# Two cross-attentions of a decoder: early key loads, row normalisation on another engine, one edge product for two batches

## The chip, the cores and the metric

The kernel runs on one core of a Trainium2 chip. It is one program of 47,756 instructions on five engines: TensorE (PE in the profile; PEld are its weight loads), VectorE (DVE), ScalarE (ACT), GpSimd (POOL) and SyncE (SP), which here only issues transfers. The metric is the time of one execution on the device in microseconds, lower is better.

## The reference

Two decoder layers work on x of 2 batches x 512 tokens x 512 features; each has self-attention, cross-attention to a context of 2 x 1024 x 512, and a mixture of experts. Every sublayer gets the layer norm of x, and its result is added to x.

```python
x = x + attn0(layernorm(x))            # 16 heads of 32, rotary, causal
x = x + xattn0(layernorm(x), ctx)
x = x + moe0(layernorm(x))             # 8 experts, best 2
x = x + attn1(layernorm(x))
x = x + xattn1(layernorm(x), ctx)
x = x + moe1(layernorm(x))             # 32 experts, best 6, and a shared one

# xattn0: 16 heads of 32. qdq rounds each row to 255 steps of its own scale
q = qdq(xn) @ qdq(wq).T + bq
k, v = split(ctx @ wkv.T + bkv)
out = qdq(softmax(q k / sqrt(32)) v) @ qdq(wp).T + bp

# xattn1: 16 heads of 128. Context rows 0..256 ("image") have their own weights
q = rms(xn @ q_w + q_b) * nq_s
k = [rms(ctx[:257] @ ki_w + ki_b) * nki_s, rms(ctx[257:] @ k_w + k_b) * nkt_s]
v = [ctx[:257] @ vi_w + vi_b, ctx[257:] @ v_w + v_b]
out = (attention over image rows + attention over text rows) @ o_w + o_b
```

## The kernel before

Each sublayer is a sequence of stages. A stage (class `Stage`, line 47) owns buffers and semaphores; leaving it clears the semaphores and sets a barrier over all engines. In a stage a block holds one hand-written program per engine; the order of the work is the order of these programs, and they meet only in semaphores. An engine that waits holds everything behind it in its program. P is 128, D 512, KC = 4 (chunks of 128 features), NT = 8 (row tiles of 128 tokens). The eight banks of PSUM are `g.ps`.

**Self-attention's output stage** (`self_attention`, 228 to 258) multiplies by wo, adds to x, and takes each row tile's mean and deviation (`g.mv`, `g.rstd`), so that a later layer norm is one instruction per tile. Its block has programs for PE, DVE and ACT only.

**First cross-attention, projections** (`project_cross0`, 873). First it calls `layer_norm` (139) with `turn=False`: a stage of its own in which DVE normalises the eight tiles into `g.xt` (line 173) and SP runs `load_first` (922): key half of wkv, context chunk 0, three biases, value half of wkv, wq, wp, context chunk 1. After its barrier comes the main block:

- PE: keys of context chunks 0 and 1 (`key`, line 1113, eight units of 4 products, four banks), after `wkv_loaded` has counted both halves of wkv; then the turns of the rounded wq and rows (1131), row scales (1144), queries (1153), values of chunks 0 and 1 (1122), the turns of wp, keys and values of chunks 2 and 3. The context sits in a ring of two chunks.
- ACT: per key unit the bias (1058) into one of two slots of `raw`, then the high part (1052); in between the rounded tiles become bf16 (`whole`, 1064): one of wq after each of the first four keys, two row tiles after each of the next four. Then it copies the turned tiles (1068).
- POOL: ones for a later pack (792), then for each unit the low part, raw minus high (976).
- SP: per unit a store of the high and of the low part (941, 943). A slot of `raw` is free only when both have landed (`held`, 1045).
- DVE: rounds wq (reduce 984, then 995 and 998 per tile), then the eight normalised tiles, then wp.

**Second cross-attention** (`cross_attention1`, 1961). Products that need full precision are done as three (`split_matmul`, 2077): both operands are split into a high part, as the reduced-precision type takes it, and the rest. `project_kq1` (2085) makes keys and queries of 16 heads in six units per head, each stored by SP (2154); POOL adds up the squares (2330). At the end SP waits until all stores have landed (2179 and 2180), then the stage closes. `project_v1` (2343) makes the values in four groups of 512 columns. Its opening: PE adds the squares over the partitions (2432, 2435), ACT takes roots (2463, 2467), then ACT splits image and text weights (2446) and DVE makes their low parts (2480). A group has 16 units of 128 context rows: four of image rows, two edge units, one per batch, and ten of text rows. The edge unit's tile holds context row 256, the last image row, and 127 text rows; the tile is multiplied by the text weights into its bank and, a second time, by the image weights into bank 4 + b, of which only the first row is used:

```python
for kind, bank in [(m, t % 4)] + ([(0, 4 + b)] if kb == EDGE else []):
    for k in range(KC):
        mm = split_matmul(...)
```

DVE adds the bias (2496), for an edge unit also the one image row (2500); ACT makes the high part (2459), POOL the low part (2523), SP stores both (2391). PE waits for DVE's row four units back, ACT for the store four units back. Before the last group SP issues the first loads of keys and queries for the attention (`load_kq`, 1979), into the buffer from which `project_kq1` stored.

## Time and profile before

| | us |
|---|---|
| Median of 3 runs (lowest, highest) | 3056.08 (3052.72, 3059.84) |
| Profiled execution, its time / its span | 3058.46 / 3056.3 |
| PE busy | 2733.5 (89% of the span) |
| PE weight loads | 2009.2 (66%) |
| DVE / ACT / POOL busy | 1484.0 / 1298.6 / 1105.3 |
| DMA | 521.87 MB, 171 GB/s on average |
| Granted PE clock, mean | 0.939 of 2.4 GHz |

The profile is of one execution. All times within it count from the span's start. In a timeline row stand the start, the length, the engine, the line of the code, the operation, what is written from what, and how often in a row; in brackets how long the engine had idled and what released it. "SPq" is the issuing of a transfer, not the transfer. A clock of 0.50 is 1.2 GHz. The matmuls overlap, so the spacing of their starts tells more than their lengths. The first cross-attention's projections run from about 282 to 432 us, the second's keys and queries from 1300 to 1595, and its values from 1595 to 1813.

### The profile page before, as it was taken

The page shows a single profiled execution, that of the slowest core. Times are in us where ns is not written, and L with a number is a line of the kernel's source. Part 1 is how long each engine was busy: PE and PEld are TensorE (multiplying, and loading weights), DVE is VectorE, ACT ScalarE, POOL GpSimd, SP SyncE. Part 2 cuts the span into 40 slices and gives each one's busy share as a digit, 9 for nine tenths or more (in the row PEclk, how much of TensorE's full clock was granted, in tenths as well). Part 3 has the DMA queues.
Part 4 walks back from the last instruction along what each step waited for, and adds up shares of the span by engine and source line. Part 5 has one row for each costly group of instructions (what it writes and reads, how often), then busy time and mean ns, then how long its engine had stood idle before and what let it go on. Part 6 is the DMA issues. An engine that isn't in the chain of part 4 may idle for free. (4 is left out here: it accounts for less than half of the span.)

```text
span 3056.3 us, 47756 instructions
## 1 busy us (share of the span) xinstructions
PE 2733.5 (89%) x15758; PEld 2009.2 (66%) x15758; DVE 1484.0 (49%) x2664; ACT 1298.6 (42%) x2923; POOL 1105.3 (36%) x1019
## 2 busy tenths in 40 slices
PE   7887899996699498889989989999998879999987
PEld 5653443432588375478877879999997647777762
DVE  5575436776211427588864337667663441111115
ACT  2462424554111136466652238888882202222220
POOL 2352225664111205335543445555551011122116
PEclk9898999998699799989999999999999889999998
DMA  2332424310499414066666764444431129999986
GB/s 93 83 84 94 154 84 100 67 32 4 171 324 321 135 42 104 23 207 244 230 233 204 213 216 171 173 172 172 176 147 59 51 67 341 344 345 344 338 257 211
DMA packets 318128, 521.87 MB, mean 171 GB/s; under 512 B 35474, under 2 KB 168466, under 8 KB 309812
## 3 DMA queue, kind: packets, MB, share of 16 engines
q1 hardware_dynamic: 290036, 450.00, 45.3%
q0 software_dynamic: 13280, 43.53, 4.6%
q10 hardware_dynamic: 14688, 26.75, 2.4%
q8 instruction: 70, 1.15, 0.2%
q14 instruction: 54, 0.44, 0.0%
HBM read 365.39 MB, written 129.50 MB: 162 GB/s over the span
## 5 line engine op out<-in xcount | busy, mean ns | idle before, releaser
L1788 PE MATMUL ps<-moe_blocks_xgt,moe_blocks_w 128*128 128x128 f32 (+1 forms) x3000 | 356.1, 278 | 9.2 <-DMA moe_blocks_b1s<-rb_cols 5.8
L1788 PEld LDWEIGHTS ps<-moe_blocks_xgt,moe_blocks_w 128*128 128x128 f32 (+1 forms) x3000 | 343.2, 185 | 13.7 <-issue 9.9
L2718 POOL TENSOR_TENSOR normed<-normed,xa_core_rinv 128x257 f32<-128x257 f32 (+1 forms) x256 | 260.4, 1039 | 214.3 <-DVE xa_core_rinv L2642 214.3
L1859 DVE COPY moe_blocks_y<-ps 128x512 f32<-128x512 f32 x102 | 70.5, 692 | 451.5 <-PE ps L1770 451.5
L1770 PE MATMUL ps<-moe_blocks_w,moe_blocks_ht 128*128 128x512 f32 (+1 forms) x612 | 279.8, 594 | 0.0
L596 POOL TENSOR_TENSOR sa_w<-sa_w,sa_core_rinv 128x256 f32<-128x256 f32 (+3 forms) x128 | 159.4, 1253 | 225.5 <-DVE sa_core_rinv L543 225.0
L1735 POOL COPY moe_blocks_idx<-moe_index 128x1 uint32 (+1 forms) x102 | 18.6, 183 | 556.0 <-PE ps L1761 428.8
L2698 ACT ACTIVATE normed<-normed,xa_core_nmax,xa_rq 128x257 f32<-128x257 f32 (+1 forms) x256 | 206.7, 809 | 4.2
L2330 POOL TENSOR_TENSOR normed<-normed 128x512 f32<-128x512 f32 x96 | 150.5, 1568 | 116.8 <-DVE normed L2283 116.8
L1809 ACT ACTIVATE moe_blocks_xgt<-ps 128x512 f32<-128x512 f32 x102 | 60.9, 597 | 299.6 <-PE ps L1761 299.6
L833 DVE TENSOR_REDUCE xa_nmax<-ps 128x1 f32<-128x1024 f32 x128 | 149.2, 1216 | 58.9 <-PE ps L824 58.9
L1770 PEld LDWEIGHTS ps<-moe_blocks_w,moe_blocks_ht 128*128 128x128 f32 (+1 forms) x612 | 109.1, 192 | 98.5 <-issue 98.5
L2657 DVE CUSTOM_DVE_ANT_0 normed<-ps,xa_rk 128x257 f32<-128x257 f32 (+1 forms) x256 | 164.6, 682 | 14.4 <-PE ps L2082 10.5
L573 ACT ACTIVATE sa_w<-ps,sa_core_nmax 128x128 f32<-128x128 f32 (+3 forms) x256 | 132.3, 523 | 82.5 <-DVE sa_core_nmax L539 81.3
L2688 ACT ACTIVATE xa_core_pt<-ps 128x512 fp32r<-128x512 f32 x256 | 139.0, 595 | 65.4 <-PE ps L2620 65.0
L2648 DVE TENSOR_TENSOR xa_core_pt<-ps,xa_core_pt 128x512 fp32r<-128x512 f32 x256 | 164.5, 684 | 3.5 <-ACT xa_core_pt L2688 3.5
L2080 PE MATMUL ps<-xa_core_pt,xa_core_v 128*128 128x256 f32 x512 | 155.5, 304 | 0.1
L498 PE MATMUL ps<-identity,sa_w 128*128 128x128 f32 x640 | 125.7, 308 | 30.8 <-DVE normed L552 16.5
L1838 ACT ACTIVATE moe_blocks_ht<-ps,moe_blocks_b1s 128x128 f32<-128x128 f32 (+1 forms) x237 | 68.9, 361 | 179.7 <-PE ps L1788 179.7
L2082 PE MATMUL ps<-xa_core_pt,xa_core_v 128*128 128x256 f32 x512 | 145.1, 283 | 0.0
L2081 PE MATMUL ps<-xa_core_pt,xa_core_v 128*128 128x256 f32 x512 | 144.9, 283 | 0.0
L2523 POOL TENSOR_TENSOR xa_v_parts<-normed,xa_v_parts 128x512 fp32r<-128x512 f32 x64 | 89.5, 1400 | 126.2 <-ACT xa_v_parts L2459 126.2
(347 smaller groups left out, 6678.0 us busy)
## 6 DMA issues: line engine op xcount, KB each, us to landing
moe_blocks_w<-L_ffn_rw SPq DMA_DIRECT2D x79, 704.0 KB, 5.7
moe_blocks_w<-L_ffn_rw SPq DMA_DIRECT2D x79, 512.0 KB, 6.8
k_parts<-xa_parts SPq DMA_DIRECT2D x64, 512.0 KB, 3.3
v_parts<-xa_v_parts SPq DMA_DIRECT2D x128, 256.0 KB, 2.7
xa_parts<-k_parts SPq DMA_DIRECT2D x32, 1024.0 KB, 6.7
xa_core_v<-v_parts SPq DMA_DIRECT2D x32, 1024.0 KB, 4.9
moe_blocks_w<-L_ffn_w SPq DMA_DIRECT2D x23, 1408.0 KB, 7.6
moe_y<-moe_blocks_y ACTq DMA_DIRECT2D x102, 256.0 KB, 6.3
```

What stands on the lines that cost most here:

```text
L596: nc.gpsimd.tensor_tensor(prob[:, 2 * s:2 * s + 2, 0:n], prob[:, 2 * s:2 * s + 2, 0:n], rinv[:, s, :, 0:1].to_broadcast([P, 2, n]), ALU.mu ...
L833: nc.vector.tensor_reduce(self.nmax[:, i % 2, m:m + 1], g.ps[:, bank:bank + 2, :].rearrange("p a n -> p (a n)"), X_AXIS, ALU.max, negate=T ...
L1770: mm = nc.tensor.matmul(g.ps[:, 6 + s % 2, :], ht[0:fn, s % 2, f, :], w2s[s][0:fn, f, :], start=(f == 0), stop=(f == NF - 1))
L1788: mm = nc.tensor.matmul(g.ps[0:fn, 2 + s % 2 + 2 * half, f * P:(f + 1) * P], w1s[s][:, k, half * F + f0:half * F + f0 + fn], xgt[:, s % 2, ...
L2080: nc.tensor.matmul(out, lhs_high, rhs_high, start=start, stop=False)
L2081: nc.tensor.matmul(out, lhs_high, rhs_low, start=False, stop=False)
L2082: return nc.tensor.matmul(out, lhs_low, rhs_high, start=False, stop=stop)
L2330: nc.gpsimd.tensor_tensor(sums[:, u * 512:(u + 1) * 512], sums[:, u * 512:(u + 1) * 512], sq[:, u % 2, :], ALU.add).then_inc(summed, 1)
L2648: nc.vector.tensor_tensor(pt[:, slot, 1, 4 * half:4 * half + 4, at:at + P], g.ps[:, 4 + half, :].rearrange("p (m q) -> p m q", m=4), pt[:, ...
L2657: ins = nc.vector.tensor_tensor_reduce(prob[:, n % PR, lo:hi], s_ps(n)[:, lo:hi], rk[:, b * CTX + lo:b * CTX + hi], 1.0, -3.4e38, ALU.mult ...
L2698: ins = nc.scalar.activation(prob[:, n % PR, lo:hi], prob[:, n % PR, lo:hi], ACT.Exp, scale=rq[:, t:t + 1], bias=nmax[:, n % PR, m:m + 1], ...
L2718: ins = nc.gpsimd.tensor_tensor(prob[:, n % PR, lo:hi], prob[:, n % PR, lo:hi], rinv[:, n % PR, m:m + 1].to_broadcast([P, hi - lo]), ALU.mult)
```

## The change

In the first cross-attention, `FirstKeys` lays the key weights and context chunk 0 into `g.xt`; SP loads them in the block of self-attention's output stage, in four transfers of 512 KB. The call of `layer_norm` is gone: the main block starts directly after that stage, SP issues the other loads at the head of its program in a new order (biases, wq, context chunk 1, value weights, wp), and POOL normalises the eight row tiles into a new buffer `xn` after its ones and ahead of the first low part; DVE waits for all eight before it takes the row maxima. PE waits for the value weights apart.

In the second, SP's waits for the stores of the keys and queries move from the end of that stage to just before `load_kq`. ACT splits the first image weights before it takes the roots. The two edge products of a group become one: its weight operand takes every 16th column of the high and low context (which are now padded by 256 zeroed columns), from row 256 of batch 0 on, so that column 0 is that row and column 64 is row 256 of batch 1; the result goes to bank 4 once per group, ahead of the first edge unit's own product, and DVE reads partitions 0 and 64.

The diff, cut:

```diff
@@ -228,6 +229,11 @@
             made, added = ou.sem("made"), ou.sem("added")
...
             with nc.Block() as block:
+                if ahead is not None:
+                    @block.sync
+                    def _(sp):
+                        ahead.load(sp)
                 @block.tensor
@@ -851,26 +857,42 @@
...
-def cross_attention0(nc, g, name, ctxt, wq, bq_cols, wkvt, bk_cols, bkv, wp, bp):
-    xn = g.xt[:, :, :].rearrange("p k (a d) -> p (k a) d", d=D)
+class FirstKeys:
+    def __init__(self, nc, g, name, ctxt, wkvt):
+        halves = g.xt[:, :, :].rearrange("p (a k) n -> p a (k n)", a=2)
+        self.w, self.ctx = [halves[:, n, :].rearrange("p (k n) -> p k n", k=KC) for n in range(2)]
+        self.src = [wkvt[:, 0:D], ctxt[:, 0:512]]
+        self.w_loaded, self.ctx_loaded = [nc.alloc_semaphore(f"{name}_{what}_ahead") for what in ("w", "ctx")]
+    def load(self, sp):
+        for k in range(0, KC, 2):
+            for dst, src, sem in ((self.w, self.src[0], self.w_loaded), (self.ctx, self.src[1], self.ctx_loaded)):
+                sp.dma_start(dst[:, k:k + 2, :], src[k * P:(k + 2) * P, :].rearrange("(k p) n -> p k n", p=P)
+                             ).then_inc(sem, 16)
+def cross_attention0(nc, g, name, ctxt, wq, bq_cols, wkvt, bk_cols, bkv, wp, bp, first):
...
+        st.sems += [first.w_loaded, first.ctx_loaded]
...
-            project_cross0(nc, g, pr, xn, ctxt, wq, bq_cols, wkvt, bk_cols, bkv, wp, ot, packs, v, wpt, wp_scale)
+            project_cross0(nc, g, pr, first, ctxt, wq, bq_cols, wkvt, bk_cols, bkv, wp, ot, packs, v, wpt, wp_scale)
...
-def project_cross0(nc, g, st, xn, ctxt, wq, bq_cols, wkvt, bk_cols, bkv, wp, spare, packs, v, wpt, wp_scale):
+def project_cross0(nc, g, st, first_keys, ctxt, wq, bq_cols, wkvt, bk_cols, bkv, wp, spare, packs, v, wpt, wp_scale):
@@ -881,8 +903,9 @@
...
-    wkv = st.sbuf("wkv", [P, KC, 2 * D])
-    ctx = st.sbuf("ctx", [P, RING, KC, 512])
+    xn = st.sbuf("xn", [P, NT, D])
+    wk, wv = first_keys.w, st.sbuf("wv", [P, KC, D])
+    ctx = [first_keys.ctx, st.sbuf("ctx1", [P, KC, 512])[:, :, :]]
@@ -916,21 +939,18 @@
...
-        sp.dma_start(ctx[:, n % RING, :, :], ctxt[:, n * 512:(n + 1) * 512].rearrange("(k p) n -> p k n", p=P)
+        sp.dma_start(ctx[n % RING], ctxt[:, n * 512:(n + 1) * 512].rearrange("(k p) n -> p k n", p=P)
...
-        sp.dma_start(wkv[:, :, 0:D], wkvt[:, 0:D].rearrange("(k p) n -> p k n", p=P)).then_inc(wkv_loaded, 16)
-        load_chunk(sp, 0)
...
-        sp.dma_start(wkv[:, :, D:2 * D], wkvt[:, D:2 * D].rearrange("(k p) n -> p k n", p=P)).then_inc(wkv_loaded, 16)
-        for n, src in enumerate((wq, wp)):
-            sp.dma_start(w_rows[n][:, :, :], src.rearrange("(c p) n -> p c n", p=P)).then_inc(w_loaded[n], 16)
+        sp.dma_start(w_rows[0][:, :, :], wq.rearrange("(c p) n -> p c n", p=P)).then_inc(w_loaded[0], 16)
...
-    layer_norm(nc, g, st.name + "_ln", turn=False, prefetch=load_first)
+        sp.dma_start(wv[:, :, :], wkvt[:, D:2 * D].rearrange("(k p) n -> p k n", p=P)).then_inc(wv_loaded, 16)
+        sp.dma_start(w_rows[1][:, :, :], wp.rearrange("(c p) n -> p c n", p=P)).then_inc(w_loaded[1], 16)
@@ -946,6 +966,7 @@
                 b, half = divmod(n, CTX // S)
...
+            load_first(sp)
             for n in range(EARLY):
@@ -969,6 +990,9 @@
         def _(pool):
             packs.put_ones(nc, 0)
             pool.wait_ge(packs.ones_done, 1)
+            for t in range(NT):
+                nc.gpsimd.tensor_scalar(xn[:, t, :], g.x[:, t, :], g.mv[:, t, 0:1], g.rstd[:, t:t + 1],
+                                        ALU.subtract, ALU.mult).then_inc(normed, 1)
             for u in range(UNITS):
                 pool.wait_ge(high_done, u + 1)
@@ -1008,6 +1032,7 @@
             dve.wait_ge(w_loaded[0], 16)
...
             nc.vector.tensor_copy(wq_scale[:, :], scale[:, 0:KC]).then_inc(bias_done, 1)
+            dve.wait_ge(normed, NT)
             round_rows(KC, NT, 1)
@@ -1132,9 +1157,11 @@
                                              jobs[n][1][:, k * P:(k + 1) * P], g.ident16[:, :])
...
-            pe.wait_ge(wkv_loaded, 32)
+            pe.wait_ge(first_keys.w_loaded, 32)
+            pe.wait_ge(ctx_loaded[0], 32)
             for n in range(EARLY):
-                pe.wait_ge(ctx_loaded[n % RING], 16)
+                if n == 1:
+                    pe.wait_ge(ctx_loaded[1], 16)
                 for c in range(KC):
@@ -1154,13 +1181,14 @@
...
+            pe.wait_ge(wv_loaded, 16)
...
-                pe.wait_ge(ctx_loaded[n % RING], 32)
+                pe.wait_ge(ctx_loaded[n % RING], 48 if n % RING == 0 else 32)
...
@@ -1981,8 +2009,8 @@
...
-            ctx_high = md.sbuf("ctx_high", [P, KC, B * CTX], F32R)
-            ctx_low = md.sbuf("ctx_low", [P, KC, B * CTX], F32R)
+            ctx_parts = [md.sbuf(f"ctx_{part}", [P, KC * B * CTX + EDGE_PAD], F32R) for part in ("high", "low")]
+            ctx_high, ctx_low = [t[:, 0:KC * B * CTX].rearrange("p (k n) -> p k n", k=KC) for t in ctx_parts]
@@ -1991,10 +2019,13 @@
...
+            stored = [md.sem(f"stored{u}") for u in range(6)]
...
-                project_kq1(nc, g, kq, a, ctx_high, ctx_low, k_dram, q_dram, rk, parts, early, load_image)
+                project_kq1(nc, g, kq, a, ctx_high, ctx_low, k_dram, q_dram, rk, parts, early, load_image, stored,
+                            [t[:, KC * B * CTX:].bitcast(F32) for t in ctx_parts])
...
-                project_v1(nc, g, vs, a, ctx_high, ctx_low, v_dram, rk, rq, minus_rq, wi, wi_loaded, load_image, load_kq)
+                project_v1(nc, g, vs, a, ctx_high, ctx_low, v_dram, rk, rq, minus_rq, wi, wi_loaded, load_image, load_kq,
+                           stored, ctx_parts)
@@ -2176,8 +2206,6 @@
...
-            for u in range(UH):
-                sp.wait_ge(stored[u], 16 * H)
@@ -2333,6 +2361,8 @@
...
+            for pad in pads:
+                nc.gpsimd.memset(pad, 0.0).then_inc(zeroed, 1)
@@ -2401,6 +2432,8 @@
             load_bias(0, 1)
...
                 group(n)
+            for done in kq_stored:
+                sp.wait_ge(done, 16 * H)
             for s in range(2):
@@ -2411,6 +2444,10 @@
...
+            def edges(ctx, k):
+                first, apart = k * B * CTX + EDGE * P, B * CTX // P
+                return ctx[:, first:first + apart * P:apart]
@@ -2421,11 +2458,13 @@
...
-                    for kind, bank in [(m, t % 4)] + ([(0, 4 + b)] if kb == EDGE else []):
+                    if t == NI:
...
-                            mm = split_matmul(nc, g.ps[:, bank, :], tile(ctx_high, m, b, kb, k), tile(ctx_low, m, b, kb, k),
-                                              w_high[:, kind, k, :], w_low[:, kind, k, :], start=(k == 0),
-                                              stop=(k == KC - 1))
+                            split_matmul(nc, g.ps[:, 4, :], edges(ctx_parts[0], k), edges(ctx_parts[1], k), w_high[:, 0, k, :],
+                                         w_low[:, 0, k, :], start=(k == 0), stop=(k == KC - 1))
+                    for k in range(KC):
+                        mm = split_matmul(nc, g.ps[:, t % 4, :], tile(ctx_high, m, b, kb, k), tile(ctx_low, m, b, kb, k),
+                                          w_high[:, m, k, :], w_low[:, m, k, :], start=(k == 0), stop=(k == KC - 1))
@@ -2458,6 +2497,7 @@
                         act.wait_ge(stored[t % RING], (UT // RING * n + t // RING) * 32)
...
+            split_weights(0, 0)
             for c in range(B * CTX // 512):
@@ -2466,7 +2506,6 @@
             act.wait_ge(eps_put, 1)
...
                                  bias=eps_q[:, 0:1]).then_inc(rooted, 1)
-            split_weights(0, 0)
             split_weights(0, 1)
@@ -2495,9 +2534,11 @@
...
+                        at = b * (P // B)
...
-                        ins = nc.vector.tensor_tensor(rows[0:1, t % 2, :], g.ps[0:1, 4 + b, :], bias[0:1, 0, :], ALU.add)
+                        ins = nc.vector.tensor_tensor(rows[0:1, t % 2, :], g.ps[at:at + 1, 4, :], bias[at:at + 1, 0, :],
+                                                      ALU.add)
```

## Rows read from the trace of the kernel before

**Rows 1.** The page, part 1: busy time of each engine over the whole span.

```profile
PE 2733.5 (89%) x15758; PEld 2009.2 (66%) x15758; DVE 1484.0 (49%) x2664; ACT 1298.6 (42%) x2923; POOL 1105.3 (36%) x1019
```

**Rows 2.** Windows, first cross-attention: length, busy us of PE, PEld, DVE, ACT, POOL; PE clock, DMA share, GB/s.

```profile
260.00:278.50 18.50, 18.50 (x44) 7.88 (x42) 8.05 (x20) 1.47 (x5) 0.00 (x0) 1.00 0.00 0
282.00:294.00 12.00, 0.21 (x1) 0.21 (x2) 6.26 (x9) 0.00 (x0) 3.51 (x1) 0.50 0.90 320
299.00:324.00 25.00, 25.00 (x64) 11.06 (x63) 19.99 (x38) 14.52 (x25) 8.93 (x7) 1.00 0.44 169
```

**Rows 3.** Timeline at the entry of the first cross-attention: start us, length, engine, line.

```profile
280.53 0.16 DVE L97 RECIPROCAL row_rstd<-sa_out_std 128x1 f32<-128x1 f32 x1 [0.31 <-ACT sa_out_std L92]
281.82 0.39 SPq L923 DMA_DIRECT2D xa_proj_wkv<-wkvt  x1
...
284.45 0.46 SPq L928 DMA_DIRECT2D xa_proj_wkv<-wkvt  x1
...
290.17 3.51 POOL L792 MEMSET xa_pk<- 2x4096 f32 x1 [43.95 <-POOLq L67]
...
293.79 6.52 PE L1113 MATMUL ps<-xa_proj_ctx,xa_proj_wkv 128*128 128x512 f32 x9 [15.29 <-DMA xa_proj_wkv<-wkvt]
```

**Rows 4.** Windows of the second cross-attention's value stage.

```profile
1602.00:1606.00 4.00, 0.66 (x6) 0.57 (x6) 1.21 (x1) 3.30 (x3) 0.00 (x0) 0.99 0.00 0
1607.00:1612.00 5.00, 4.86 (x11) 3.81 (x12) 2.57 (x4) 0.00 (x0) 0.00 (x0) 0.50 0.63 216
1664.00:1713.00 49.00, 49.00 (x218) 40.61 (x217) 16.78 (x21) 13.62 (x18) 23.54 (x17) 1.00 0.76 226
```

**Rows 5.** DMA issues, 281.5 to 282.2 and 300 to 330: count, KB each, us to landing.

```profile
xa_proj_wkv<-wkvt SPq DMA_DIRECT2D x1, 1024.0 KB, 5.1
...
xa_k_parts<-xa_proj_low SPq DMA_DIRECT2D x8, 256.0 KB, 2.0
```

**Rows 6.** Timeline of the first cross-attention's keys and rounding.

```profile
301.49 1.30 POOL L976 TENSOR_TENSOR xa_proj_low<-xa_proj_raw,xa_proj_high 128x512 fp32r<-128x512 f32 x1 [7.81 <-ACT xa_proj_high L1052]
301.69 1.37 DVE L998 TENSOR_SCALAR xa_proj_rounded<-xa_proj_rounded 128x512 f32<-128x512 f32 x1
...
303.49 0.43 DVE L998 TENSOR_SCALAR xa_proj_rounded<-xa_proj_rounded 128x512 f32<-128x512 f32 x1
...
323.96 0.69 ACT L1058 ACTIVATE xa_proj_raw<-ps,xa_proj_bks 128x512 f32<-128x512 f32 x1 [1.05 <-PE ps L1113]
...
325.21 1.13 ACT L1064 ACTIVATE xa_ot<-xa_proj_rounded 128x512 bf16<-128x512 f32 x2
```

**Rows 7.** POOL, groups by form: instruction, count, busy us, mean ns, idle before.

```profile
L596 POOL TENSOR_TENSOR sa_w<-sa_w,sa_core_rinv 128x512 f32<-128x512 f32 x32 | 33.3, 1040 | 28.6 <-DVE sa_core_rinv L543 28.6
...
L2028 POOL TENSOR_TENSOR residual<-residual,xa_out_bo 128x512 f32<-128x512 f32 x8 | 12.9, 1647 | 22.1 <-DMA xa_out_bo<-L_xattn_o_b 22.1
...
L2334 POOL MEMSET normed<- 128x3072 f32 x1 | 2.7, 2667 | 58.1 <-DVE xa_kq_x_low L2305 58.1
```

**Rows 8.** Timeline from the keys to the values, second cross-attention.

```profile
1589.12 3.05 SPq L2154 DMA_DIRECT2D q_parts<-xa_parts  x2
...
1591.28 1.64 POOL L2330 TENSOR_TENSOR normed<-normed 128x512 f32<-128x512 f32 x1 [1.07 <-DVE normed L2283]
1595.49 0.40 SPq L2375 DMA_DIRECT2D xa_v_wt<-L_xattn_v_w  x1
...
1600.82 1.84 PE L2435 MATMUL ps<-all_ones,normed 128*128 128x1 f32 x16
...
1604.79 2.29 DVE L2480 TENSOR_TENSOR xa_v_w_low<-xa_made_early,xa_v_w_high 128x2048 fp32r<-128x2048 f32 x1 [9.18 <-ACT xa_v_w_high L2446]
...
1607.14 0.80 PE L2080 MATMUL ps<-xa_v_w_high,xa_made_ctx_high 128*128 128x512 f32 x1 [4.48 <-DVE xa_v_w_low L2480]
```

**Rows 9.** Weight loads (PEld), groups by form over the whole span.

```profile
L2081 PEld LDWEIGHTS ps<-xa_v_w_low,xa_made_ctx_high 128*128 128x128 f32 x288 | 54.8, 190 | 11.5
...
L1400 PEld LDWEIGHTS ps<-moe_loads_w,normed 128*128 128x128 f32 x128 | 25.2, 308 | 8.5 <-issue 8.5
```

More of the change, by code:

```diff
@@ L31 @@
 NIMG = 257
+EDGE_PAD = NIMG // P * P
 LN_EPS = 1e-5
@@ L198, in _, with self_attention @@
                     mm.then_inc(turned, 1)
-def self_attention(nc, g, name, wqkv, wo, rope, mask):
+def self_attention(nc, g, name, wqkv, wo, rope, mask, ahead=None):
     with Stage(nc, name) as st:
@@ L902, in project_cross0 @@
     w_loaded = [st.sem("wq_loaded"), st.sem("wp_loaded")]
-    wkv_loaded, b_loaded = st.sem("wkv_loaded"), st.sem("b_loaded")
-    ctx_loaded = [st.sem(f"ctx_loaded{n}") for n in range(RING)]
+    wv_loaded, b_loaded, normed = st.sem("wv_loaded"), st.sem("b_loaded"), st.sem("normed")
+    ctx_loaded = [first_keys.ctx_loaded, st.sem("ctx1_loaded")]
     tops, scaled, inverted, shifted, clipped = (st.sem("tops"), st.sem("scaled"), st.sem("inverted"),
@@ L1112, in key @@
                 for k in range(KC):
-                    mm = nc.tensor.matmul(g.ps[:, m % 4, :], wkv[:, k, c * P:(c + 1) * P], ctx[:, n % RING, k, :],
+                    mm = nc.tensor.matmul(g.ps[:, m % 4, :], wk[:, k, c * P:(c + 1) * P], ctx[n % RING][:, k, :],
                                           start=(k == 0), stop=(k == KC - 1))
@@ L1121, in value @@
                 for k in range(KC):
-                    mm = nc.tensor.matmul(g.ps[:, 4 + m % 2, :], ctx[:, n % RING, k, t * P:(t + 1) * P],
-                                          wkv[:, k, D:2 * D], start=(k == 0), stop=(k == KC - 1))
+                    mm = nc.tensor.matmul(g.ps[:, 4 + m % 2, :], ctx[n % RING][:, k, t * P:(t + 1) * P],
+                                          wv[:, k, :], start=(k == 0), stop=(k == KC - 1))
                 mm.then_inc(v_made, 1)
@@ L2082, in split_matmul, with project_kq1 @@
     return nc.tensor.matmul(out, lhs_low, rhs_high, start=False, stop=stop)
-def project_kq1(nc, g, st, a, ctx_high, ctx_low, k_dram, q_dram, rk, parts_out, early, load_image):
+def project_kq1(nc, g, st, a, ctx_high, ctx_low, k_dram, q_dram, rk, parts_out, early, load_image, stored, pads):
     UH, RR = 6, 4
@@ L2114, in project_kq1 @@
     squared, summed, zeroed = st.sem("squared"), st.sem("summed"), st.sem("zeroed")
-    stored = [st.sem(f"stored{n}") for n in range(UH)]
     scaled = st.sem("scaled")
@@ L2340, in _, with project_v1 @@
                 head(i, 1)
-def project_v1(nc, g, st, a, ctx_high, ctx_low, v_dram, rk, rq, minus_rq, wi, wi_loaded, load_image, load_kq):
+def project_v1(nc, g, st, a, ctx_high, ctx_low, v_dram, rk, rq, minus_rq, wi, wi_loaded, load_image, load_kq,
+               kq_stored, ctx_parts):
     NKT = CTX // P
@@ L2752, in decoder_kernel @@
         if 1 in stages:
-            self_attention(nc, g, "sa0", a["wqkv0"], a["wo0"], (a["cos"], a["sin"], a["swap"]), a["mask"])
+            first = FirstKeys(nc, g, "xa0", a["ctxt"], a["wkvt0"])
+            self_attention(nc, g, "sa0", a["wqkv0"], a["wo0"], (a["cos"], a["sin"], a["swap"]), a["mask"], first)
         if 2 in stages:
@@ L2756, in decoder_kernel @@
                              a["bk0_cols"], a["L0_xattn_bkv"],
-                             a["L0_xattn_wp"], a["L0_xattn_bp"])
+                             a["L0_xattn_wp"], a["L0_xattn_bp"], first)
         if 3 in stages:
```

## The prediction

> **What bounds the kernel now.** I read the page first: TensorE (PE) is busy for 89% of the span, VectorE (DVE) for half, the rest less [rows 1]. So time is won in two ways only: PE works where it now stands, or it has fewer instructions where it never stands. The windows of the stretches that the change touches say which is which. In the entry of the first cross-attention, 282 to 294 us, PE is busy 0.2 us in 12 while the DMA engines are 90% busy; from 299 to 324 it never stops [rows 2]. The timeline of the entry gives the chain: the previous stage's last DVE instruction ends at 280.69; after a barrier, at 281.8, the loads are issued and DVE normalises the rows; the next block opens at 290.2 (POOL's memset), and PE begins its first key at 293.79, released by the load of wkv: it waits for both halves of it, and the second was issued at 284.45 [rows 3]. In the second cross-attention's value stage PE works without a hole, at the full clock, after an opening at the 1.2 GHz level [rows 4].
>
> **Part 1, the entry of the first cross-attention.** Removed: the layer norm's block with its barrier, and the wait for 2 MB of key weights and context. These are now issued in the previous stage's last block, beside its projection, where the DMA engines are idle (share 0.00 from 260 to 278.5 [rows 2]). One MB as the first of a queue landed 5.1 us after its issue [rows 5], so 2 MB are there in time, and four issues instead of two cost nothing on an idle SP. PE's first key can start when the block opens, 281.9 instead of 293.79: **11.9 us**. The slow clock stays a cost of the same size: the old kernel's first nine records lasted 6.5 us after an idle stretch of 15 [rows 3]. The clock, full until 278.5, was already at half by 282 [rows 2], so I expect the new start at 1.2 GHz too, with a microsecond or two either way.
>
> What is late next? The 11.9 us count only if ACT, which interleaves each key's bias and high part with the rounding copies, finishes as much earlier. It takes the eighth key at 323.96, and its last rounding copy before the turns ends at 326.34 [rows 6]. Three things feed it:
> (a) Loads. wq is now SP's fourth DMA, issued at about 283.4; with 5.1 us it lands at 288.5. The three ahead of it are small. Context chunk 1 is the next, due when PE has made four keys, not before 296; the engines moved 320 GB/s at a share of 0.90 [rows 2], so 1 MB more takes 3 us, and it lands at 292. The value weights and wp come last and nobody asks for them before 325. The first stores queue behind these 4 MB, which are through by about 298; that can cost one store a microsecond.
> (b) POOL: a memset of 3.5 us [rows 3], then eight normalisations of 128x512. No row shows this instruction on POOL. Below it, a memset of 128x3072 took 2.67 us, 0.44 per 512 columns; the nearest is a product of one full operand with a broadcast value, 1.04; above it an addition of two operands, 1.65 [rows 7]. I take 1.04: POOL is free at 281.9 + 3.5 + 8.3 = 293.7. The first key's low part queues behind that, and ACT may overwrite a ring slot only when its low part is stored. A round of a slot is 1.4 us (two passes of ACT at 0.69 or a little less, rows 6), 1.3 (POOL, rows 6), 0.3 (issue), 2.0 (landing, rows 5) and about 0.4 of handing over: 5.4 us for every second key. The first low part is made at 295.0 and stored at 297.4; so keys 2, 4 and 6 are taken at 297.4, 302.8, 308.2, and key 7 at about 310.7. PE makes its eighth key at 324.0 - 11.9 = 312.1, so POOL has about 1 us in hand at this price.
> (c) DVE: the row maxima now wait for POOL, 293.7, but wq's rounding keeps DVE until about 298. A rounding pass takes 0.43 us, and took 1.37 with a POOL instruction of 1.30 beside it [rows 6]; three or four will meet the normalisation, and POOL may be held as often by 0.4.
> The Trainium skill has a rule for that (SBUF — State Buffer, the part on the two sides of SBUF): the port pair of VectorE and GpSimd is an exclusive lock for a whole instruction, and the loser blocks. By the rows above the trace agrees.
> For (a) to (c) I take 0.9 off: part 1 is worth **11 us**; 7.9 at 1.65 per normalisation (8 x 0.61 = 4.9 later, 1 of it in hand, of 11.9), 12.9 if nothing is lost and the clock rises early. The turns, the queries and the rest of the stage are released by ACT's end and shift with it.
>
> **Part 2, from keys to values in the second cross-attention.** SP's wait for the last stores goes. SP had issued the last at 1592.17, POOL ended at 1592.92, yet the next block opened at 1595.49 [rows 8]; a barrier alone cost 281.82 - 280.69 = 1.13 [rows 3]. So it can open at 1594.1: **1.4 us**. The waits now stand ahead of SP's loads for the last value group, some 150 us later, when all is stored: nothing.
> ACT now splits the image weights before the roots. Before, PE made its sums until 1602.66, the split came after the last root, and DVE's low part of 2.29 us after the split let PE begin at 1607.14 [rows 8]. Now both are done some 4.4 us after the opening, while PE's sums take 7.2, and PE goes on at once: **4.5 us**. The text weights' split still follows the last root; it is due at the fifth unit, 10.8 us after the first. DVE's first row comes after it, some 5 us into the units; with four banks PE needs that row at the fifth unit too: hidden.
> Without that hole I expect no fall of the clock: it was full from 1602 to 1606, at half from 1607 to 1612, and 11 products there took 4.86 us [rows 4], 0.44 each against 0.22. Twelve of them: **2.6 us**, or nothing if the clock falls all the same. Two small memsets on an idle POOL: nothing.
>
> **Part 3, one edge product.** A group has 16 units of 12 products and two edge products of 12: 216. In the window of one group PE never leaves 218 products in 49.00 us, 0.225 each [rows 4]. Now 204: 12 x 4 groups x 0.225 = **10.8 us**. DVE's edge additions stay eight. But the edge product's weight load now takes columns 64 bytes apart; 48 such loads. No row shows one. A contiguous load takes 0.190 us and hides under the product before it; under that there is no gain. The dearest full load is 0.308 on average [rows 9]; twice the contiguous one, 0.38, would add 48 x 0.155 = 7.4 us. I take the contiguous row, which is nearest in kind, hence nothing, and keep 7.4 for the range.
> The Trainium skill speaks against this (SBUF — State Buffer, the note on cachelines): a line has 16 bytes, and an access pattern that crosses to a new line each time pays a penalty; it gives no figure, and no run here shows it yet. By it the gain shrinks by whatever the load exceeds 0.225.
>
> **Sum.** 11 + 1.4 + 4.5 + 2.6 + 10.8 = 30.3 us. The profiled execution took 3058.46 us (its span of 3056.3 and 2.2 around it), which would become 3028.2; it lies 2.4 above the median 3056.08 of the three runs, and for a median I forecast **3026 us**.
>
> **Rivals.**
> A. POOL becomes the bound of part 1. At 2.5 us per normalisation it is free 11.7 us later, and 10.7 of the 11.9 are lost: gain 19.3 + 1.2, **3036**. For it: the row is missing. Against: the dearest of 512 columns in rows 7 is 1.65.
> B. The spread weight load takes 0.38: gain 22.9, **3033**. For it: the load fills 0.19 of 0.225 already. Against: nothing in the trace.
> C. Stores bound the value stage, and what the edge product frees is given back: gain 19.5, **3037**. For it: a DMA share of 0.76 in a full group [rows 4], in bursts. Against: 0.76 x 216 / 204 is 0.80, and PE never stood in that group.
> D. Slower: the spread load is very dear. The place is the edge product of each group; it eats the whole 30.3 us at 0.225 + 30.3 / 48 = 0.86 us, 4.5 times the contiguous load; at 1.0 it costs 37.2, **3063**. For it: only the missing row. Against: no group of rows 9 is near it.
>
> **How the numbers follow.** Forecast 0.62, A 0.09, B 0.14, C 0.07, D 0.03, and 0.05 for a spread load near break-even or two rivals together. The forecast's own range is 3020 to 3032. Low end 3020: 12.9 in part 1, and the runs' spread of 3.5 us to a side. High end 3041: 7.9 in part 1, 7.4 for the loads and no gain of clock leave 17.2, with a little for the spread. What a measurement can tell from no change is 0.2%, 6 us. Faster 0.91, same 0.04, slower 0.05.
>
> **What would show it.** PE's first key at about 282, its eighth near 312, ACT's last rounding copy near 315, POOL's normalisations at 1.04; the value block opening 1.2 us after POOL's last addition, no hole between PE's sums and the first value product, and full clock there; 816 value products, 46 us per group; the edge product's loads at 0.19. It is wrong if POOL's rows are over 1.3, if SP still ends the keys' stage, or if products of the edge stand over 0.23 us apart.

## The result, and the profile after

The changed kernel took **3034.34 us** (median of 5 runs, 3030.19 to 3039.12); the kernel before, on the same chip, 3056.08 (3051.19 to 3059.84). The ratio is 0.9932, 95% interval 0.992 to 0.9945: 16.8 to 24.4 us faster. The profiled execution was the fastest of the five, 3030.19 us with a span of 3028.4.

The page, part 1, and the windows that answer to [rows 2, 4]:

```profile
PE 2718.4 (90%) x15710; PEld 1996.4 (66%) x15710; DVE 1479.4 (49%) x2656; ACT 1297.6 (43%) x2923; POOL 1123.5 (37%) x1029
```

```profile
260.00:278.50 18.50, 18.00 (x42) 7.61 (x40) 8.53 (x21) 1.47 (x5) 0.00 (x0) 1.00 0.01 6
282.00:294.00 12.00, 12.00 (x25) 5.15 (x24) 5.33 (x11) 1.81 (x3) 11.89 (x6) 0.86 0.91 306
299.00:324.00 25.00, 15.39 (x44) 6.73 (x42) 17.50 (x28) 14.31 (x25) 13.60 (x10) 0.86 0.41 157
1594.00:1606.00 12.00, 12.00 (x61) 9.97 (x60) 5.14 (x7) 5.17 (x7) 2.53 (x2) 1.00 0.65 207
1648.11:1694.41 46.30, 46.30 (x206) 38.79 (x205) 16.66 (x21) 13.62 (x18) 23.41 (x17) 1.00 0.80 238
```

PE issued 48 products fewer. From 282 to 294 it now works all the time where it had worked 0.21 us. But look at the next window: from 299 to 324 it had never stopped, and now it is busy 15.4 us of 25. Most of what was won at the entry was lost again before the stage was half done. The last two windows are as forecast: no hole at the opening of the value stage, full clock, a group of 204 products in 46.30 us.

The timeline of the changed kernel says what PE waited for, indirectly: ScalarE's and VectorE's rows beside GpSimd's (start, length, engine, line).

```profile
281.51 15.67 PE L1138 MATMUL ps<-normed 128*128 128x512 f32 x32 [3.52 <-PEq L68]
...
284.94 17.45 POOL L994 TENSOR_SCALAR xa_proj_xn<-residual,row_mv,row_rstd 128x512 f32<-128x512 f32 x8
302.36 2.49 POOL L1000 TENSOR_TENSOR xa_proj_low<-xa_proj_raw,xa_proj_high 128x512 fp32r<-128x512 f32 x2
...
302.42 4.84 DVE L1008 TENSOR_REDUCE xa_proj_top<-xa_proj_xn 128x1 f32<-128x512 f32 x8 [5.10 <-POOL xa_proj_xn L994]
...
305.76 0.69 ACT L1083 ACTIVATE xa_proj_raw<-ps,xa_proj_bks 128x512 f32<-128x512 f32 x1 [9.87 <-DMA xa_k_parts<-xa_proj_low]
...
306.50 8.83 PE L1138 MATMUL ps<-xa_proj_ctx,normed 128*128 128x512 f32 x16 [2.45 <-ACT xa_proj_raw L1083]
...
310.56 0.69 ACT L1083 ACTIVATE xa_proj_raw<-ps,xa_proj_bks 128x512 f32<-128x512 f32 x1 [1.17 <-DMA xa_k_parts<-xa_proj_low]
...
321.64 0.63 ACT L1089 ACTIVATE xa_ot<-xa_proj_rounded 128x512 bf16<-128x512 f32 x1 [1.13 <-DVE xa_proj_rounded L1022]
...
322.90 1.07 PE L1156 MATMUL ps<-identity,xa_proj_wq_int 128*128 128x128 bf16 x8 [7.13 <-ACT xa_proj_wqt L1093]
```

PE had six of its eight keys made at 304.05 (a key is four products, and each of these is two records in the profile). Four of them had not been taken and filled the banks, since ScalarE took the third only at 305.76: it needed the ring slot whose low part GpSimd made from 302.36 on, behind eight normalisations of 2.18 us each. PE stood 2.45 us there, and 7.13 us more after its eighth key, for ScalarE's first copy of a turned tile, which follows the last rounding copy. ScalarE's last rounding copy ends at 322.27, against 326.34 [rows 6]. Counted from the opening of the main block (281.32) or of the first block of before (281.82), that is 40.95 instead of 44.52: a gain of 3.6. The whole projection stage, to the opening of the core, shrank from 168.2 to 162.9.

The passage to the value stage, and its opening, against [rows 8]:

```profile
1586.32 1.64 POOL L2358 TENSOR_TENSOR normed<-normed 128x512 f32<-128x512 f32 x1 [1.07 <-DVE normed L2311]
...
1588.78 0.40 SPq L2406 DMA_DIRECT2D xa_v_wt<-L_xattn_v_w  x1
...
1594.58 1.84 PE L2474 MATMUL ps<-all_ones,normed 128*128 128x1 f32 x16
...
1596.28 0.48 PE L2111 MATMUL ps<-xa_v_w_high,xa_made_ctx_high 128*128 128x512 f32 x1
```

The block opens 0.82 us after GpSimd's last addition ended (2.57 before), and the products follow the sums without a gap. From opening to the opening of the attention core the stage took 200.7 us; it had taken 217.8. So the trace puts **5.3** to the first cross-attention, **1.7** to the wait and **17.1** to the value stage, 24.1 in all, inside the measured interval.

These are single profiles, and the profiles of the experiments show how far to trust them. In seven others with the same value stage it took 199.9 to 201.7 us. In six others with this projection stage (experiments 3, there but for one wait, 4, 6, 7, 8 and 11) the last rounding copy ended 40.7 to 41.2 us after the opening, so 3.6 is firm, but the stage took from 161.8 to 164.9, so the 5.3 is good to 2 us or so. What the stage gained behind the copy is in part the granted clock. PE waits there about 3 us for VectorE to take values, and then ran its next 6 us at 0.50 before, at 0.72 in the changed kernel, and at 1.00 in experiment 6, whose projection stage has the same code (in this order):

```profile
354.00:360.00 6.00, 5.85 (x7) 2.53 (x8) 0.70 (x2) 2.58 (x4) 3.18 (x3) 0.50 0.57 220
349.50:355.50 6.00, 5.95 (x10) 2.60 (x11) 1.11 (x2) 2.71 (x4) 3.08 (x3) 0.72 0.57 220
350.55:356.55 6.00, 6.00 (x14) 2.76 (x15) 1.23 (x2) 2.59 (x4) 3.03 (x3) 1.00 0.57 220
```

### The profile page after: what moved, and what is told of

Read it like the earlier page. It is cut to its first block and busy times, and to the rows that moved or that the text cites. A ratio compares the mean times of both kernels' runs of the same rounds, so it can differ in the third digit from the quotient of the medians.

```text
span 3028.4 us, 47640 instructions
## 1 busy us (share of the span) xinstructions
PE 2718.4 (90%) x15710; PEld 1996.4 (66%) x15710; DVE 1479.4 (49%) x2656; ACT 1297.6 (43%) x2923; POOL 1123.5 (37%) x1029
## 5 line engine op out<-in xcount | busy, mean ns | idle before, releaser
L1816 PEld LDWEIGHTS ps<-moe_blocks_xgt,moe_blocks_w 128*128 128x128 f32 (+1 forms) x3000 | 341.3, 184 | 10.8 <-issue 8.4
L2111 PE MATMUL ps<-xa_made_ctx_high,xa_kq_w_high 128*128 128x256 f32 (+2 forms) x384 | 124.5, 324 | 12.5 <-DVE xa_made_ctx_low L2329 9.8
```

The costliest lines, as they stand in the source:

```text
L1816: mm = nc.tensor.matmul(g.ps[0:fn, 2 + s % 2 + 2 * half, f * P:(f + 1) * P], w1s[s][:, k, half * F + f0:half * F + f0 + fn], xgt[:, s % 2, ...
L2111: nc.tensor.matmul(out, lhs_high, rhs_high, start=start, stop=False)
```

## The experiments

Times are medians; each set ran beside the kernel before on one chip, and ratios are to it. For the first three, the clearest reading is how long after the opening of the main block ScalarE ends its last rounding copy.

**1. Normalisation on VectorE, early.** The eight instructions move from GpSimd's list to the head of VectorE's:

```
-                nc.gpsimd.tensor_scalar(xn[:, t, :], ...)      # POOL, after the memset
+                nc.vector.tensor_scalar(xn[:, t, :], ...)      # DVE, ahead of wait_ge(b_loaded, 48)
```

> VectorE normalises the eight row blocks at the head of the block, while it waits for wq (it idled 6.2 and 2.1 us there); GpSimd does its memset and then only low parts. In the changed kernel GpSimd's eight normalisations took 17.45 us (2.19 each), first low part at 302.4, VectorE's row maxima began at 302.42, ScalarE's last rounding copy ended at 322.3. Both theories of the loss expect the same here: maxima begin at about 297.2 (wq's rounding ends), last rounding copy near 316, stage end 5 to 6 us sooner, 3029 us. If the loss is not GpSimd's at all (loads, the clock), nothing moves: 3034.

Measured: **3028.56 us** (3026.58 to 3034.2), ratio 0.9907 (0.9891 to 0.9922). The last rounding copy ends at 315.94, 34.25 after the opening of 281.69; the stage took 158.0. GpSimd's normalisations cost 6.7 us at that copy, 4.8 in the whole stage and 5.8 by the medians. Five rows of its timeline:

```profile
281.69 3.51 POOL L798 MEMSET xa_pk<- 2x4096 f32 x1 [35.61 <-POOLq L68]
...
281.73 6.93 DVE L1028 TENSOR_SCALAR xa_proj_xn<-residual,row_mv,row_rstd 128x512 f32<-128x512 f32 x8 [1.18 <-PEq L68]
...
299.22 0.69 ACT L1083 ACTIVATE xa_proj_raw<-ps,xa_proj_bks 128x512 f32<-128x512 f32 x1 [3.14 <-DMA xa_k_parts<-xa_proj_low]
...
304.03 0.69 ACT L1083 ACTIVATE xa_proj_raw<-ps,xa_proj_bks 128x512 f32<-128x512 f32 x1 [0.67 <-DMA xa_k_parts<-xa_proj_low]
...
315.31 0.63 ACT L1089 ACTIVATE xa_ot<-xa_proj_rounded 128x512 bf16<-128x512 f32 x1 [1.14 <-DVE xa_proj_rounded L1019]
```

**2. Normalisation on VectorE, late.** The same, with the eight instructions behind wq's rounding. GpSimd is free, VectorE's maxima are nearly as late as in the changed kernel.

> VectorE normalises too, but only after wq's rounding, at 297.2, so its row maxima begin at about 301.1, nearly as late as in the changed kernel (302.4), while GpSimd is free for low parts from 284.9. Theory R (the ring: late low parts, hence late stores, hold ScalarE's keys, and that is the bound; it is the mechanism of rival A of the prediction): as good as the kernel with early normalisation, about 3029. Theory D (VectorE's own chain is the bound: 19.1 us of maxima and rounding passes that start when the last row is normalised, and the ring has slack): only 1.3 us better than the changed kernel, 3033, last rounding copy at about 321.

Measured: **3028.75 us** (3027.05 to 3029.28), ratio 0.9903 (0.9888 to 0.9917). Theory R had this right. The maxima began at 301.80, and yet the last rounding copy ends at 318.53, 36.2 after the opening: 4.7 us of the 6.7 come back (4.2 of the 4.8 in the stage) though VectorE's chain begins only 1.6 us sooner relative to the opening. The 2 us that are missing are VectorE's: ScalarE, done with the fifth key, now waits 2.62 us for the first rounded rows.

```profile
301.80 4.84 DVE L1005 TENSOR_REDUCE xa_proj_top<-xa_proj_xn 128x1 f32<-128x512 f32 x8
...
308.96 0.63 ACT L1089 ACTIVATE xa_ot<-xa_proj_rounded 128x512 bf16<-128x512 f32 x1 [2.62 <-DVE xa_proj_rounded L1019]
...
317.40 1.13 ACT L1089 ACTIVATE xa_ot<-xa_proj_rounded 128x512 bf16<-128x512 f32 x2
```

**3. Normalisation on GpSimd, but VectorE waits row block by row block.**

```
-            dve.wait_ge(normed, NT)
+                    if group == 1: dve.wait_ge(normed, j - first + 1)   # before each maximum
```

> GpSimd normalises as in the changed kernel (until 302.4), but VectorE waits for each row block before that block's maximum instead of for all eight before the first. Its maxima can start at 297.2 and the last ends 0.6 after 302.4: the chain is 4.2 us sooner; GpSimd's low parts stay late. Theory D: 4 us better than the changed kernel, 3030, last rounding copy at about 318. Theory R: nothing, 3034, as ScalarE gets its third key at 305.8 all the same. Something between if the two bind in turn.

Measured: **3033.71 us** (3032.48 to 3035.85), ratio 0.992 (0.9906 to 0.9934), the same as the changed kernel. VectorE ended its maxima 4 us sooner and then stood, for ScalarE; ScalarE's last copy ends 41.1 after the opening, where it was (40.95).

```profile
307.29 0.99 DVE L1021 TENSOR_SCALAR xa_proj_rounded<-xa_proj_xn,xa_proj_inv 128x512 f32<-128x512 f32 x1 [3.85 <-ACT xa_proj_wq_int L1090]
...
310.11 0.69 ACT L1084 ACTIVATE xa_proj_raw<-ps,xa_proj_bks 128x512 f32<-128x512 f32 x1 [1.18 <-DMA xa_k_parts<-xa_proj_low]
```

Experiments 2 and 3 together settle the cause: free GpSimd with VectorE late, and most comes back; free VectorE with GpSimd late, and nothing does. It is the ring (low part, store, slot), not VectorE's wait for the normalised rows. The fifth key shows it best. ScalarE takes it 29.24 us after the opening in the changed kernel, 29.38 in this experiment and 22.34 in experiment 1, and from there to the last rounding copy it needs 11.7, 11.7 and 11.9. In that last part the ring no longer sets the pace: ScalarE waits 1.1 us twice for VectorE's rounding (the row of 321.64 is one of the two). In the changed kernel's trace alone VectorE's chain looks as likely a cause, since it runs without a long stall from 302.42 to the end; both chains start when GpSimd ends its last normalisation, and only moving one at a time tells which holds.

**4 and 5. The parts alone.** The kernel before with part 1 only, and with parts 2 and 3 only.

> The kernel before with the first part of the change alone (loads a stage ahead, rows normalised on GpSimd); the second cross-attention as before. The traces put 5.3 us to this part: 3051. The prediction had 11: 3045.

> The kernel before with the second and third part alone (waits for the stores moved, image weights split ahead of the roots, one edge product); the first cross-attention as before. If the parts add up: 17.1 us of value stage and 1.7 of opening, 3037. If the clock or the stores tie the parts together, less.

Measured: **3051.85 us** (3048.57 to 3056.89), ratio 0.998 (0.9971 to 0.999), and **3041.06 us** (3037.61 to 3043.74), ratio 0.9952 (0.994 to 0.9965). By the ratios 6 us and 15 us, together the 21 that the whole change gave: the parts add up. In the trace of the first the projection stage took 163.7 us, 4.5 less than before. In the trace of the second, value stage (201.1) and wait are shorter by 18.5 us, while its interval ends at 18.3; what the few microseconds between are stays open.

**6. Two edge products, as before**, in the changed kernel (contiguous weight loads, 216 products per group).

> The changed kernel with the two contiguous edge products of before in each group instead of the one with a step of 64 bytes. By 12 x 4 x 0.227 us: 10.9 slower, less 0.5 for the weight loads that are contiguous again: 10.4, 3045; group of 49.0 us. If stores had bound the value stage (rival C) it would cost less than 8.

Measured: **3043.1 us** (3041.78 to 3048.28), ratio 0.9963 (0.995 to 0.9976), 8.8 above the changed kernel. The value stage took 211.55 us in its trace, 10.9 more. Nothing was given back to the stores: rival C is out.

**7. The edge product's weights from neighbouring columns.**

```
-                return ctx[:, first:first + apart * P:apart]
+                return ctx[:, first:first + P]
```

> The changed kernel with the edge product's weights read from 128 neighbouring columns instead of every 16th (the values of the edge tokens are then not the right ones: that part of the output is left out). Prices the spread load: 48 products at 0.236 instead of 0.227 each in the trace of the changed kernel, 0.5 us in all, so 3034; if the load were as dear as rival B had it (0.38), 7 us better.

Measured: **3032.49 us** (3030.24 to 3035.4), ratio 0.9924 (0.9911 to 0.9937): not to be told from the changed kernel. The weight loads differ, though. First the changed kernel: two of the twelve spread loads, then the product beneath which the first of them runs, and the last of the twelve products:

```profile
1653.65 0.30 PEld L2112 LDWEIGHTS ps<-xa_v_w_low,xa_made_ctx_high 128*128 128x128 f32 x1
1653.89 0.30 PEld L2113 LDWEIGHTS ps<-xa_v_w_high,xa_made_ctx_low 128*128 128x128 f32 x1
```

```profile
1653.41 0.40 PE L2113 MATMUL ps<-xa_v_w_high,xa_made_ctx_low 128*128 128x512 f32 x1
...
1656.24 0.39 PE L2113 MATMUL ps<-xa_v_w_high,xa_made_ctx_low 128*128 128x512 f32 x1
```

Then the groups of loads of the value stage, the changed kernel's and the one with neighbouring columns (count, busy us, mean ns, idle before):

```profile
L2112 PEld LDWEIGHTS ps<-xa_v_w_low,xa_made_ctx_high 128*128 128x128 f32 x272 | 52.9, 194 | 9.9
```

```profile
L2112 PEld LDWEIGHTS ps<-xa_v_w_low,xa_made_ctx_high 128*128 128x128 f32 x272 | 51.1, 188 | 10.5
```

A spread load takes 0.30 us, a contiguous one 0.19. Yet the twelve products of an edge unit stand 2.83 / 12 = 0.236 us apart, against 46.30 / 204 = 0.227: 0.1 us per group, 0.4 in all. The records of such loads (0.30 long, 0.24 apart) overlap each other, so a load longer than the product above it did not hold PE for the difference.

**8. The image weights split after the roots, as before.**

```
-            split_weights(0, 0)          # ahead of the roots
             for c in range(B * CTX // 512): ... Sqrt
+            split_weights(0, 0)
             split_weights(0, 1)
```

> The changed kernel with ScalarE splitting the image weights after the roots, as before. By the prediction's terms the hole of 4.5 us comes back, and with it 2.6 us of half clock: 7 us slower, 3041. If the clock falls or stays for another reason, 4.5 alone: 3039.

Measured: **3040.79 us** (3037.11 to 3049.77), ratio 0.9954 (0.9939 to 0.9968), 6.5 above the changed kernel; value stage 207.5, 6.8 more. The hole is back to the hundredth [rows 8], and with it the lower level; the first and the ninth product behind it, and a window:

```profile
1603.42 0.79 PE L2111 MATMUL ps<-xa_v_w_high,xa_made_ctx_high 128*128 128x512 f32 x1 [4.48 <-DVE xa_v_w_low L2519]
...
1606.87 0.40 PE L2113 MATMUL ps<-xa_v_w_high,xa_made_ctx_low 128*128 128x512 f32 x1
```

```profile
1603.00:1608.00 5.00, 4.58 (x13) 3.67 (x14) 2.85 (x4) 0.00 (x0) 0.00 (x0) 0.63 0.66 221
```

Eight products take 3.45 us here (1603.42 to 1606.87) where they would take 1.8 at 0.227 each: the lower level cost 1.6. With the 4.5 of the hole that is 6.1 of the 6.8; the rest is no more than the 1.8 us by which this stage differs between profiles of the same code. In the kernel before the lower level lasted longer behind the same hole: thirteen products from 1607.14 to 1612.83, 2.7 us lost (the prediction had 2.6). So the hole cost a third to over a half as much again at the lower level.

**9. Value weights and wp behind the stores**, with normalisation early on VectorE.

```
-        sp.dma_start(wv ...), sp.dma_start(w_rows[1] ...)    # 2 MB, ahead of the stores
+                    load_late(sp, KC * n + c)               # 256 KB behind each key's stores
```

> As the kernel with early normalisation on VectorE (3028.6), and SP loads the value weights and wp, which nobody needs before 325, in eight pieces of 256 KB, one behind each of the first eight keys' stores, instead of 2 MB ahead of them. In that kernel the first low part's store was issued at 289.94 behind 3 to 4 MB of loads, and ScalarE's third key waited for it until 299.22 (3.14 us idle). If those loads are what is left of the loss, the third key is taken at about 296.1 and the store lands some 3 us after its issue; VectorE's chain (its maxima begin at 297.6 all the same) then binds, and 1 to 2 us come out: 3027, last rounding copy 1 to 2 us sooner. If the 2 MB cost nothing, 3028.6 again. If the pieces get in the way of later stores, slower: 3030.

Measured: **3030.07 us** (3025.15 to 3037.47), ratio 0.9917 (0.9903 to 0.993). The mechanism is there: ScalarE takes its third key without a stall, 14.35 us after the opening of 282.42 (17.53 in experiment 1, the row of 299.22). The gain is not: the last copy ends 33.95 after the opening (34.25 there), since ScalarE now waits 2.62 us for VectorE's rounding. GpSimd's third low part now runs at 298.17 and meets VectorE's copy of wq's scales, 1.23 us instead of 0.16, and the maxima behind it begin 17.1 after the opening instead of 15.9. By its time the kernel can't be told from experiment 1; its projection stage took 155.9 us, 2.2 less, within the 3 us by which that stage differs between profiles of the same code.

```profile
296.77 0.67 ACT L1089 ACTIVATE xa_proj_raw<-ps,xa_proj_bks 128x512 f32<-128x512 f32 x1
...
298.35 1.23 DVE L1040 COPY xa_proj_wq_scale<-xa_proj_scale 128x4 f32<-128x4 f32 x1
...
315.24 1.13 ACT L1095 ACTIVATE xa_ot<-xa_proj_rounded 128x512 bf16<-128x512 f32 x2
```

**10. Prices on GpSimd.** A single profile, four instructions of each form; the rest as in the changed kernel.

> The changed kernel with twenty more instructions on GpSimd ahead of its normalisations, four of each form, VectorE waiting for them: the same tensor_scalar with two per-row operands, with one per-row operand, with two immediates, a tensor_tensor with the per-row operand broadcast (1.04 us in the rows that the prediction leaned on), and the two-operand form over 256 columns. It prices the forms. If the two per-row operands are what costs, the first is 2.19 and the others 1.0 to 1.3; if tensor_scalar is slow on GpSimd whatever its operands, the second and third are near 2.2 or 1.6 and the broadcast form near 1.0; if the cost is per instruction, the 256 columns take over 1.5, if it is per column, 1.1.

Measured (count, busy us, mean ns; all on an otherwise quiet port, VectorE waiting):

```profile
L995 POOL TENSOR_SCALAR xa_proj_xn<-residual,row_mv,row_rstd 128x512 f32<-128x512 f32 x4 | 8.2, 2071 | 0.1
L1003 POOL TENSOR_SCALAR xa_proj_xn<-residual 128x512 f32<-128x512 f32 x4 | 7.6, 1923 | 0.1
L999 POOL TENSOR_SCALAR xa_proj_xn<-residual,row_mv 128x512 f32<-128x512 f32 x4 | 6.2, 1563 | 0.1
L1011 POOL TENSOR_SCALAR xa_proj_xn<-residual,row_mv,row_rstd 128x256 f32<-128x256 f32 x4 | 4.8, 1215 | 0.1
L1007 POOL TENSOR_TENSOR xa_proj_xn<-residual,row_mv 128x512 f32<-128x512 f32 x4 | 4.0, 1038 | 0.1
```

Tensor_scalar is slow there whatever its operands: immediates (1.92) cost nearly what per-row values do (2.07). It is not the number of operands read from memory either: the form with a broadcast operand reads as much and takes 1.04. Halving the columns takes 0.86 off, so 3.3 ns a column and 0.36 fixed. By these prices one instruction with two operators costs as much as two broadcast instructions would; that form was not run as a normalisation. Beside VectorE's work, in the changed kernel, a normalisation took 2.18.

**11. SP's wait for the last stores back.** A single profile.

> The changed kernel with SP's wait for the last stores of keys and queries back at the end of that stage. The prediction had 1.4 us for it. In the changed kernel the value block opened 0.8 us after GpSimd's last addition, in the kernel before 2.6 after. So: it opens 2.2 to 2.6 us after that addition; 1.4 to 1.8 us in the trace, too little for the times of single runs.

Measured: the block opens 2.53 us after GpSimd's last addition ended (1588.50), against 0.82 without the wait: 1.7 us. The single time, 3037.14, says nothing.

```profile
1586.86 1.64 POOL L2360 TENSOR_TENSOR normed<-normed 128x512 f32<-128x512 f32 x1 [1.07 <-DVE normed L2313]
...
1591.03 0.40 SPq L2408 DMA_DIRECT2D xa_v_wt<-L_xattn_v_w  x1
```

## Why the prediction was right, and where it was not

It said 3026 us and it was 3034.3, inside the range of 3020 to 3041 and outside the forecast's own, 3020 to 3032. The sum was 30.3 us; the traces show 24.1. One term carries the difference. That the time still fell inside the range is in part luck: its high end allowed for 7.9 us from part 1 at worst, and part 1 gave 5.3; it held because it also allowed 7.4 us for the spread loads and 2.6 for the clock, which were not lost. Of the prediction's own signs of being wrong two came: GpSimd's normalisations took over 1.3 us (2.18), and the edge products stood over 0.23 us apart (0.236). The first cost half of part 1, the second 0.4 us.

- **First key at 282**: right, 281.51. The loads a stage ahead landed in time and hid.
- **The slow clock stays a cost of the same size**: it was smaller. The granted clock was 0.66 on average over the first 3.5 us of PE's keys, a mix of the two levels of 1.2 and 2.4 GHz, and full from 290 on (windows of the changed kernel below); PE had idled 3.5 us before. In the kernel before the first nine records, after 15 us of idling, had lasted 6.5 us [rows 3]. Nothing came of it, since PE stood later for ScalarE.

```profile
281.51:285.00 3.49, 3.49 (x6) 1.51 (x7) 0.00 (x0) 0.00 (x0) 3.38 (x2) 0.66 0.47 85
285.00:290.00 5.00, 5.00 (x12) 2.20 (x11) 1.50 (x3) 1.32 (x2) 5.00 (x3) 0.90 1.01 367
290.00:297.00 7.00, 7.00 (x17) 3.04 (x16) 6.30 (x13) 2.36 (x4) 7.00 (x4) 1.00 1.00 368
```

- **Step (b), a normalisation on GpSimd at 1.04 us**: this is the term that failed. It took 2.18, above the upper bound of 1.65 as well. I had taken rows of another instruction, tensor_tensor, as ends for tensor_scalar [rows 7]; experiment 10 shows that the form, which no row of before had on GpSimd, costs twice the nearest one. A bound from other forms was no bound. Rival A had the mechanism and, at 2.5 us, nearly the price: with 2.18 in its sum GpSimd is free 9.1 us late, 8.1 of the 11.9 are lost, and 3.8 are left; ScalarE's last copy showed 3.6 (the whole stage 5.3, for which see the section on the result). It deserved more than its 0.09.
- **The ring of 5.4 us per slot round as the way the loss travels**: right, by experiments 2 and 3. With GpSimd free, ScalarE's last copy ended at 315.94 where the prediction had "near 315", and the stage gained 10.1 against the 11 forecast.
- **Step (a), the stores behind 4 MB of loads, "a microsecond"**: undersized. In experiment 1 the first low part's store was issued at 289.94 and held ScalarE until 299.22, 3.1 us of stall. Experiment 9 removed it for no gain, because VectorE's chain was as late: ScalarE then waits 2.62 us for it.
- **Step (c), VectorE's maxima wait for GpSimd only until 293.7**: wrong with the price, 302.42; but experiment 3 shows that it cost nothing of its own.
- **Wait for the stores, 1.4**: 1.7. **Hole, 4.5, and clock, 2.6**: 4.5 and 2.7 in the kernel before, 1.6 for the clock when experiment 8 brought the hole back. **Edge product, 10.8**: 10.9 in the stage.
- **The spread weight load, 0.19 taken, 0.38 the other end**: it took 0.30, so rival B was nearer on the load; but B's way of turning a load's length into time failed, and 0.4 us in all were lost, not the 3.6 to 7.4 that 0.30 to 0.38 less the spacing of 0.225 give. D and C did not happen.

The profiled spans differ by 27.9 us, 4 more than the three stages account for. It lies in stages that the change does not touch: the second MoE's blocks took 475.2 us before, from the first to the last record of their code, 470.7 in the changed kernel, and between 470.3 and 480.4 in the profiles of the experiments. I count that as spread from run to run. The other way went its routing part: 91.6 to 92.6 us, from its first record to the first of the blocks, in all profiles of kernels with parts 2 and 3, whole or with one piece put back, and 90.4 in the two without them. Why was not tried.

The best version is experiment 1, or 2, which can't be told from it: 3028.6 us, the change with the normalisation left on VectorE. It beats both kernels, the changed one narrowly: the interval of experiment 2 (up to 0.9917) ends just below that of the changed kernel (from 0.992), that of experiment 1 (up to 0.9922) overlaps it. But on one chip the slowest of experiment 2's six times, 3029.28, lies below the fastest of experiment 3's six, 3032.48, and experiment 3 times like the changed kernel.

## What to carry to other kernels

Before moving work to another engine, find a row of the same instruction on that engine; a row of the same size but another form is neither a price nor a bound, and here the error of 1.1 us times eight took half of the part's gain. Where an engine gets new work ahead of its old, ask which ring or slot its old work frees, since the loss appears on the engine that waits for the slot, as a wait for a DMA. And when one event releases two chains, free them one at a time: the trace names a releaser for each, but not which one decides.

## What the runs showed of the hardware

- GpSimd's tensor_scalar over 128x512 fp32 took 2.07 us with two per-row values, 1.92 with two immediates, 1.56 with one value, against 1.04 for a tensor_tensor with the value broadcast and 0.47 for the same normalisation on VectorE (3.74 for eight, in experiment 2).
- Those eight took 6.93 us in experiment 1, beside GpSimd's memset of 3.51 us: 3.2 us more, nearly the memset's whole length. The Trainium skill's rule of a port pair that is held for a whole instruction (SBUF — State Buffer, the part on the two sides of SBUF) describes this.
- A weight load with a step of 64 bytes took 0.30 us instead of 0.19, and its products stood 0.236 us apart instead of 0.227. The Trainium skill's note that each cross to a new 16-byte line pays a penalty (SBUF — State Buffer, the note on cachelines) holds for the load; the time between products hardly saw it.
- After the hole of 4.5 us PE's clock was at the lower level for thirteen products (5.7 us) in the kernel before and for eight (3.5 us) in experiment 8; without the hole it stayed at 1.00.
- The same code did not get the same clock each time: over the 6 us after a wait of about 3 us in the first cross-attention, 0.72 in the changed kernel and 1.00 in experiment 6.
